# First lookups of a graph-attention layer: every group of score columns from TensorE, and row gathers that begin later

## The reference, cut to what matters

```
feat = (x @ W).reshape(n, 8, 64)
el = einsum('nhd,hd->nh', feat, attn_l);  er = einsum('nhd,hd->nh', feat, attn_r)
e  = leaky_relu(el[src] + er[dst], 0.2)          # 100000 edges x 8 heads
m  = segment_max(e, dst);  ex = exp(e - m[dst])
out = segment_sum(ex / denom[dst] * feat[src], dst)
```

## Time and profile before

| what | value |
|---|---|
| median of the runs | 3279.8 us |
| profiled execution, first to last instruction (span) | 3272.4 us |
| PE busy | 2624.1 us (80%) |
| DVE busy | 2317.7 us (71%) |
| ACT busy | 1279.7 us (39%) |
| POOL busy | 1066.1 us (33%) |

### The profile page before, as it was taken

How to read it: one execution, slowest core, us unless ns; L and a number is a source line. 1 busy time by engine, 2 the same in 40 slices (tenths; PEclk the granted TensorE clock), 3 DMA queues, 4 the chain that set the end, 5 groups by cost and what they waited for, 6 DMA issues and landing times.

```text
span 3272.4 us, 51000 instructions
## 1 busy us (share of the span) xinstructions
PE 2624.1 (80%) x17803; PEld 1952.4 (60%) x17803; DVE 2317.7 (71%) x3106; ACT 1279.7 (39%) x3089; POOL 1066.1 (33%) x1299
## 2 busy tenths in 40 slices
PE   5777777999899997285888888777677677876999
PEld 3666664545455554265777777555555555674888
DVE  7999997796334443288788787966666666785786
ACT  7888884020001112001444444444544454503443
POOL 3000000111102225530566666666666665003000
PEclk8999999999899998597999999899988999967999
DMA  4444446434477872031677766666666666061543
GB/s 134 183 181 177 167 182 240 123 113 134 143 262 255 261 253 89 15 106 53 181 194 193 198 190 184 179 186 186 184 184 189 184 184 190 12 200 54 158 155 112
DMA packets 316172, 537.23 MB, mean 164 GB/s; under 512 B 114066, under 2 KB 219044, under 8 KB 315668
## 3 DMA queue, kind: packets, MB, share of 16 engines
q1 hardware_dynamic: 244724, 308.43, 28.8%
q0 software_dynamic: 71200, 225.54, 24.7%
HBM read 419.84 MB, written 115.21 MB: 164 GB/s over the span
## 4 chain that ended last, share of the span: by engine, by line
PE 53%; DVE 28%; issue 7%; another core or an unknown queue 5%; ACT 5%; DMA 1%; POOL 1%; DVEq 0%; ACTq 0%; SPq 0%; POOLq 0%
PE ps L1718 20%; PE ps L1499 14%; PE ps L1706 8%; DVE a L590 8%; PE ps L1635 4%; DVE a L585 3%; DVE a L586 3%; PE ps L1405 2%; DVE a L1165 2%; DVE a L836 2%; ACT oht L1370 2%; DVE a L862 1%; ACT oh L1372 1%; PE ps L1633 1%
## 5 line engine op out<-in xcount | busy, mean ns | idle before, releaser
L1718 PE MATMUL ps<-a,oh 128*128 128x260 f32 x2008 | 508.8, 408 | 133.2 <-DVE a L1177 55.1
L1827 POOL DMA_INDIRECT a<-t,mid x502 | 486.7, 969 | 376.9 <-PE ps L1718 140.3
L1370 ACT ACTIVATE oht<-iota,mid 128x128 f32<-128x128 f32 x830 | 333.3, 402 | 627.0 <-PE ps L1718 396.4
L1499 PE MATMUL ps<-a 128*128 128x512 f32 x1200 | 555.4, 602 | 13.4 <-DVE a L769 13.4
L1718 PEld LDWEIGHTS ps<-a,oh 128*128 128x128 f32 x2008 | 389.7, 201 | 233.7 <-ACT oh L1372 97.3
L1165 DVE TENSOR_TENSOR a<-a,ps 128x520 f32 x415 | 286.3, 690 | 290.3 <-PE ps L1718 193.5
L1718 PE MATMUL ps<-wts,oh 128*128 128x260 f32 x1312 | 342.8, 416 | 115.2 <-DVE wts L1177 42.7
L1466 PE MATMUL ps<-a 128*128 128x200 bf16 x1568 | 320.4, 255 | 108.7 <-issue 51.1
L1827 POOL DMA_INDIRECT wts<-t,mid x328 | 313.5, 956 | 178.8 <-issue 82.9
L1718 PEld LDWEIGHTS ps<-wts,oh 128*128 128x128 f32 x1312 | 261.4, 206 | 184.4 <-ACT oh L1372 77.6
L1499 PEld LDWEIGHTS ps<-a 128*128 128x128 f32 x1200 | 218.8, 192 | 221.8 <-issue 215.4
(11 more groups left out here) (329 smaller groups left out, 3910.5 us busy)
## 6 DMA issues: line engine op xcount, KB each, us to landing
a<-at_d SPq DMA_DIRECT2D x60, 1280.0 KB, 6.1
at_d<-a SPq DMA_DIRECT2D x49, 800.0 KB, 3.3
mt_d<-a SPq DMA_DIRECT2D x49, 800.0 KB, 4.9
a<-mt_d SPq DMA_DIRECT2D x30, 1280.0 KB, 6.1
a<-trlo_d SPq DMA_DIRECT2D x49, 512.0 KB
ot_d<-a SPq DMA_DIRECT2D x49, 320.0 KB, 5.9
a<-ot_d SPq DMA_DIRECT2D x49, 256.0 KB, 3.3
a<-t,mid POOLq DMA_INDIRECT x502
```

The lines of the kernel that those rows point to most:

```text
L1370: e.activation(oht[:, k, :], iota[:, :], ACT.Abs, bias=ndl[:, k, s:s + 1]).then_inc(*own.inc())
L1499: m = e.matmul(acc[f].rearrange("p (x d) -> p x d", x=8), X[:, hi, P * f:P * (f + 1)], a, start=(hi == 0), stop=end, skip_group_check=True)
L1718: t = e.matmul(pbig[b][:, 512 * u:512 * u + 260], oh[:, so, k, :], hrows[2 * r + k][:, 260 * u:260 * (u + 1)], start=(k == 0), stop=(k == 1))
L1827: e.indirect_dma_start(out=hrows[2 * r + k], out_offset=None, in_=t2, in_offset=bass.IndirectOffsetOnAxis(ap=srci[:, k, s:s + 1], axis=0)) ...
```

## The change

Every group is looked up by TensorE: `FETCHED` is gone, with the table copy in DRAM, its 25 writes, the 64 gathers, their index copy on VectorE and the wait for them. The first half has 98 lookups, the second 98 as before. The row gathers of slots 0 to 9 wait for the carried maxima of the first half (`cin`, 0) where they waited for lookup 40. In a stage much earlier (64 to 531 us), two waits on a register's value get the register by an explicit maximum with 1.

```diff
-FETCHED = range(20, 24)
-GROUPS = {8: [g_ for g_ in range(NG) if g_ not in FETCHED], 1: list(range(NG))}
+GROUPS = {8: list(range(NG)), 1: list(range(NG))}
...
-        123: ["gather rows2"], 120: ["fetched"], 127: ["rf2 src"], 130: ["rf2 dst"], 134: ["slots2"]}
+        123: ["gather rows2"], 127: ["rf2 src"], 130: ["rf2 dst"], 134: ["slots2"]}
...
-        el_d = dram("el_d", [NP, 8])
-        src_f = sb("src_f", [P, 16 * len(FETCHED)], I32)
-        el_out, el_in = sem("el_out"), sem("el_in")
...
-                elif kind == "fetched":
-                    e.tensor_copy(src_f[:, :], src_n[:, 16 * FETCHED[0]:16 * FETCHED[-1] + 16]).then_inc(*V.inc("fetched sources"))
...
-                e.wait_ge(el_in, 16 * 16 * len(FETCHED))
                 for _ in leaky(0, 292, JH):
...
+            ends = e.alloc_register("pair_end")
...
-                e.wait_ge(slot_done, e.snap(ereg[p % 4], min_val=1, max_val=S))
+                e.reg_alu(ends, ereg[p % 4], 1, ALU.max)
+                e.wait_ge(slot_done, ends)
...
+            free = e.alloc_register("free_at")
...
-                    e.wait_ge(window_free, e.snap(freg[s // 8 % 4], donate=True, min_val=1, max_val=NPAIR + 8))
+                    e.reg_alu(free, freg[s // 8 % 4], 1, ALU.max)
+                    e.wait_ge(window_free, free)
...
-            e.wait_ge(el_out, 16 * NB)
-            e.wait_ge(*V("fetched sources"))
-            for n in range(16 * len(FETCHED)):
-                c = 16 * FETCHED[0] + n
-                e.indirect_dma_start(out=elv[:, 8 * c:8 * c + 8], out_offset=None, in_=el_d,
-                                     in_offset=bass.IndirectOffsetOnAxis(ap=src_f[:, n:n + 1], axis=0)).then_inc(el_in, 16)
-            e.wait_ge(*V("found", 8, 40))
+            e.wait_ge(*V("cin", 0))
             for s in range(NR):
                 gather_heads(s)
...
-                        e.wait_ge(*V("elr", o))
-                        e.dma_start(el_d[ORDER[o] * P:(ORDER[o] + 1) * P, :], elr[:, ORDER[o], 0:8]).then_inc(el_out, 16)
```

## The result

The changed kernel took 3222.0 us (median of four runs, 3221.8 to 3227.6) beside 3279.6 us for the kernel before (four runs, 3279.1 to 3280.0): 0.9828 of its time [0.9814, 0.9842], that is 57.6 us less. 3219 was forecast.

The account below looks back on a forecast made before the run. TensorE was taken to be held up one instruction at a time while gathers were in flight, neither bandwidth nor arithmetic binding. -76.5 - 14.0 + 21 + 9 = -60.5 from span 3272.4 gives 3211.9, plus 7.4: 3219 us, range 3203 to 3243.

Parts of the forecast that it names:

- the sign: Whole kernel: the change makes it faster, given 0.95; slower had 0.03 to 0.04 and no telling difference 0.02.
- The hold of the gathers, -76.5: First lookups, 1292.1 to 1372.8 us: TensorE's stall goes with the 64 gathers of `el`, -76.5 us (bounds -79.6 and -73).
- rival B: First lookups: the stall comes with them, not the gathers, so it stays and the change is slower, 3296 us; chance 0.05.
- many gathers in flight keep TensorE from being fed: Both stalls, 1292.1 to 1372.8 and 1450.4 to 1464.2 us: reading behind terms of -76.5 and -14.0 us.
- Second hold and 16 lookups, +7: First half's lookups: moving row gathers removes a stall near 1450 us, -14.0; 16 more lookups at its end cost +21.
- Late start, +9: From `cin` to slot 0: 20 gathers and both clears must now fit in, slot 0 9.0 us later (bounds 0 and 22.5).
- at 2.07 + 0.30 = 2.37 that makes 7.2 gathers: After `cin`: beside VectorE's two-input operations, which fill 17.0 us, each row gather takes 2.37 us.
- Registers, 0 with +6 as bound: Stage of the two register waits: 196 new TensorE moves cost 0, or +6 us if TensorE had no slack.
- The slots and all that follows keep their order and just come earlier: Slot 0 to the end: distance as before, 1717 us within 6, a term of 0.
- the clock would stay at its upper level: TensorE's clock, listed as a sign with lookup 6 reduced before 1300 us: stays at 2.4 GHz.
- A: Before slot 0: moved row gathers stall TensorE there too, slot 0 25.4 us late instead of 9, 3235 us; chance 0.16.
- C's hidden start: From `cin` to slot 0: gathers at 1.25 us hide the late start, a 3.35 us wait goes, 3207 us; chance 0.11.

Follow-up runs that it names:

- the registers kernel: The kernel before with only its two register waits changed to an explicit maximum, against the kernel before: 2980.2 us, 1.0010.
- the two pairs elsewhere: Row gathers waiting for `cin` against waiting for lookup 40: in the change, 3007.9 against 2998.7 us; in the kernel before with register maxima, 2987.0 against 2980.2.
- The experiment with the clears first: The changed kernel with GpSimd's two clears put between the wait for `cin` and the row gathers: 3001.3 us, 1.0085 against the kernel before.
- that with the wait at the last lookup: The changed kernel with its row gathers released by the last lookup of the first half, not `cin`: 3002.5 us, 1.0077 against the kernel before.

## Why the prediction came out

The forecast of 3219 us is 3.0 us under the measured 3222.0, and some of that closeness is luck. By the spans it missed 6.9 us (3211.9 forecast, 3218.8 measured): 12.3 us that I had put at nothing, less 5.4 us by which the other terms were too dear. The 7.4 us between span and median, which were 3.2 after the change, then took 4 us off the miss. And the sign held because this comparison was one in which the kernel before had the hold; on chip 10 the change is slower.

*The hold of the gathers, -76.5: right in size (-77.0), and its cause only half shown.* The changed kernel does the first lookups with the same instructions, the same transfer of `er` beside them, and no hold, in the comparison where the kernel before had it. So rival B's story, that the hold belongs to the first lookups themselves, is wrong, and something that the change took out or replaced was needed for it. The gathers weren't sufficient: every kernel that keeps them on the other chips has no hold. Nor are they shown to be what was needed. The change also took out the writes of `el_d` and replaced the two register waits, and no run on the first chip parts the three. For the gathers speaks that the three stretches of this kind that I found on the first chip ahead of slot 0, two before and the short one after, lie beside gathers or end just after them, and that the short one came with the registers already changed. My sentence "many gathers in flight keep TensorE from being fed" was worded as a behaviour of the kernel; it is a reading of that one comparison. That one and the same kernel could run so differently, I had not thought of; on chip 10, where the change ran again, it turns the sign of the forecast. One more thing stays open: the trace of before on the first chip holds 21.9 thousand records of semaphore updates, that of the registers kernel 40.3 thousand, so the recording wasn't the same, and I can't exclude that it has a part in the hold. Against that, the changed kernel's trace of the same comparison holds as few (21.8 thousand) and shows no such stretch but the short one before slot 0.

In the page's slice of 1309 to 1391 us PE and DVE both stand at 2 tenths, not at the 4 and 3 that I had read; the stages of the earlier trace rows, on which the term rests, are as given.

On the rule of the Trainium skill ("Runtime: NRT & Kernel Launch", Instruction fetch mechanics) that fetching is hidden: in 1284 to 1366 us the page's row of that queue has 1 block in the hold and 6 in the registers kernel, which runs at pace. The registers kernel's row (blocks, MB, share):

```profile
q8 instruction: 6, 0.10, 0.5%
```

So six blocks in 82 us are hidden, by this trace. The one block of the hold fits that TensorE used few instructions; the count is a result of the hold and says nothing on its cause. I had taken it as evidence against the rule, which it isn't.

*Second hold and 16 lookups, +7: right (+5.4).* The clean measurement of the lookups alone comes from chip 10, 20.8 us by the traces (first scan to `cin`) and 20.9 by the medians, for +21. On the first chip that leaves 5.4 - 20.8 = -15.4 for the second hold, where -14.0 was forecast; this last is a difference between chips, so an estimate.

*Late start, +9: too large by 3.* It measured +5.7 on the first chip, and +5.3 in each of the two pairs elsewhere (39.0 us less 33.7). The step at fault is "at 2.07 + 0.30 = 2.37 that makes 7.2 gathers" in the first 17 us: I took a row beside `L915` for `L951`'s operation of the same number of inputs. The groups by line of 1450 to 1490 (count, busy, mean ns, idle before):

```profile
L1824 POOL DMA_INDIRECT a<-t,mid x12 | 16.2, 1350 | 171.2 <-DVE cin L940 167.8 <-issue 3.4
L945 DVE SCALAR_TENSOR_TENSOR a<-a,cin 128x391 f32<-128x391 f32 x16 | 13.5, 920 | 0.1
L1824 POOL DMA_INDIRECT wts<-t,mid x8 | 7.6, 946 | 2.4 <-issue 2.4
```

The first twelve gathers, ten of them beside those operations, took 1350 ns on average with 0.30 between them, the last eight 946: 12 x 1.65 + 8 x 1.25 = 29.8 us, not 33.9. The other side of the sum, VectorE unslowed, held: 13.49 us for its 16 operations, 13.48 without gathers beside them. Of the rule in the Trainium skill ("SBUF — State Buffer", Who interferes with whom), the case shows that the GpSimd side waits, by 0.3 to 0.5 us a gather and once by 1.4; that VectorE is blocked when it is the second to start, which would have put the forecast 8 us later, it doesn't show. The experiment with the clears first names what the late start was made of, and that with the wait at the last lookup shows that a start 13 us before `cin` removes it.

*Registers, 0 with +6 as bound: 3, between the two.* Its interval nearly reaches 0.

*"The slots and all that follows keep their order and just come earlier": wrong by 12.3 us, the largest miss.* It is the step of the prediction that failed, a term put at nothing. The order holds: the same counts in the stage (4740 matmuls, 1101 of VectorE, 810 of GpSimd). Of the 12.3 us 6.8 lie in the slots, 4.0 between them and the next layer's first matmuls, and 1.5 behind these. Here are the slot stage of the kernel before and the first 100 us of it:

```profile
1555.40:2791.80 1236.40, 964.16 (x4740) 774.48 (x4740) 889.30 (x1101) 587.29 (x1646) 776.74 (x810) 0.94 0.68 186
1555.40:1655.40 100.00, 88.18 (x563) 74.70 (x563) 80.30 (x98) 45.51 (x128) 60.48 (x64) 1.00 0.67 186
```

and the first 100 us of it after the change:

```profile
1489.50:1589.50 100.00, 89.30 (x541) 76.05 (x542) 78.07 (x96) 44.89 (x127) 58.57 (x62) 0.93 0.66 181
```

In the stage TensorE is busy 974.2 us for 964.2 with as many matmuls, VectorE and ScalarE the same to 0.2%, and the granted clock is 0.93 for 0.94; in the first 100 us it is 0.93 for 1.00, and 22 matmuls fewer get done. So the time lost in the slots is TensorE's, and it goes with the clock. I had forecast that the clock would stay at its upper level; it does until 1435 us, but falls in the 54 us up to slot 0 (0.75, then 0.62 in the stages above), in which TensorE has 148 matmuls. That stretch is no cause by itself, for the kernel before had one like it between its last lookup of the first half and slot 0:

```profile
1507.00:1555.40 48.40, 14.57 (x132) 13.03 (x129) 42.53 (x55) 8.59 (x18) 5.60 (x1) 0.65 0.15 48
```

A part goes with the late row gathers: in the 100 us from slot 0 the four kernels with early gathers on the other chips show a clock of 1.00 (650 matmuls with the registers alone), the six with later ones 0.97 or 0.98 (639 in the change). But it is small there: slot 0 to the end takes 1517.3 us in the change for 1515.9 with the registers alone, 1.4 us more. Why it is 12.3 us on the first chip stays open.

*The rivals.* A was there in part: TensorE idle by "issue" before slot 0 and VectorE waiting for it. It came at the tail of the gathers, as its argument said, but it was short, and it ended together with the clears. C's hidden start didn't come: no trace in which gathers and then clears wait for `cin` has less than 5.3 us for it. B's mechanism is refuted where the hold was, and its sign, slower, is what the change is on the chips that have no hold; the lookups, the late start and the registers make up the 30.8 us there.

## What to carry to other kernels

A stall by "issue", with neither bandwidth nor arithmetic behind it, may not belong to the kernel: here it was in one comparison and on none of three other chips. Before work is moved onto a busy engine to avoid such a stall, count what it costs where there is none: here 64 gathers on an idle engine hid 16 lookups, 21 us. And when a queue's start is put later, look at what stands at its end: the clears, which needed nothing from the wait, were what slot 0 waited for.

## What the runs showed of the hardware

The same kernel takes 3280 us in the first comparison and 2977 to 2978 on three other chips. The stages up to 1200 us agree (from 1000 to 1200 TensorE is busy for all 200.00 us, with 604 matmuls before and 601 to 604 in four traces of chip 8). The spans of the kernel before on the first chip and of the registers alone on chip 10 are 294 us apart: 93 lie before slot 0, nearly all in the holds (77.8 and 15.4), 182 in the slots, 19 behind. The slots move 186 GB/s on one and 218 on the other, at a clock of 0.94 and 0.99.

An indirect gather of 128 rows costs GpSimd 0.95 us and 0.30 before the next, whether a row has 32 bytes or 2080 (the 946 ns above). Beside VectorE's operations over two SBUF tensors it is 1.3 to 1.5 us, in a few cases 2.0 to 2.3, and those operations take no longer for it (13.49 us for sixteen, 13.48 without).
